# Attention on pairs of heads, with float32 weights and a column of ones in the first layer

## The chip, the cores and the metric

The kernel runs on one core of one Trainium2 chip. The metric is the device time of one execution in microseconds (us), the median of several runs. The engines are TensorE (PE for its matmuls, PEld for its weight loads), VectorE (DVE), ScalarE (ACT), GpSimd (POOL) and SyncE (SP, which issues DMAs). They run their own instruction streams and meet at semaphores.

## The reference, cut to what matters

Two layers, each a cross attention and a mixture of experts, over 8 batches of 112 tokens with 256 channels. The attention looks at 375 context tokens of 192 channels. Both attentions have 16 heads.

```python
# layer 0: 16 heads of 16 channels; scores are clamped to +-10000
q, k, v = y @ Wq + bq, ctx @ Wk + bk, ctx @ Wv + bv
s = clip(q_h @ k_h.T * 0.25, -CLAMP, CLAMP)
o_h = softmax(s) @ v_h
x = x + tanh(g) * (concat(o_h) @ Wo + bo)
# layer 1: 16 heads of 64 channels, low-rank additions to the four weights;
# the last 4 context tokens have their own keys, values and softmax,
# and their result is added to that of the other 371
```

## The kernel before

Activations and weights are kept as pairs of float16 values, a high and a low part ("hi" and "lo"), and a product is made of three matmuls, hi·hi, hi·lo and lo·hi (`PARTS`). ACT writes the high part out of PSUM (a copy to float16), DVE the low part (PSUM minus the high part).

The span has these stages: set-up and weight cutting, attention of layer 0, its experts, weights of layer 1, attention of layer 1, its experts. `attention_tensor` (L537), `attention_scalar` (L688), `attention_vector` (L771) and `attention_gpsimd` (L914) are called once for each layer, and each writes out by hand one engine's order of work. The loop is over batches, and inside it over the 16 heads. For a head:

- `scores` (L603): PE makes the 112x375 scores (371 in layer 1) in three matmuls (L613) into one of two PSUM banks, `SB_[st % 2]`. The contraction runs over all 128 partitions. In layer 0 one tile of keys holds 8 heads of 16 channels, so the queries of a head lie in `qz` with zeros for the other seven heads; POOL writes them (`masks`, L917, four multiplications by a mask for each batch, L921). In layer 1 one tile holds two heads and the other half of the rows is zero.
- `maxima` (L835): in layer 0 DVE clamps the scores into `SC` and takes the extreme value along (L844), and clips once more (L847). In layer 1 it only takes the negated maximum (L850).
- `exps` (L719): ACT makes the exponentials into `P_` (float32) and sums them along (L728; the sum is a second instruction, ACTIVATION_READ_ACCUMULATOR). In layer 1 POOL then writes the 4 values of the special tokens beside them (L939).
- `turn` (L617): PE transposes the 112x375 float32 values in three pieces of 125 keys (L623), two heads after `scores`.
- `hi` (L732) and `lo` (L853): ACT and DVE cut the transposed values to a high and a low float16 part (L736, L855).
- `weigh` (L627): PE multiplies each piece, both parts, with the high and low values of the head side by side (L640), six matmuls a head, three heads after `scores`.
- `normalise` (L859): when a group of heads is done (all 16 in layer 0, four in layer 1), DVE adds the halves and multiplies by the reciprocal of the sum (L866 to L874).

Beside the heads stand "units" (`Layer.steps`), the work on the next batch's queries ("q"), keys ("k"), values ("v") and, in layer 1, special tokens ("i"), and on the last batch's result (transposes "t", product "o"). The table in `Layer.__init__` says behind which head each unit stands. A unit is PE's matmuls into one of the two banks `GB` (L558 for q, with the bias in one-row matmuls L564 in layer 0; L570 for k; L576 for v; L584 for i; L591 for t; L597 and the one-row bias L600 for o), and then ACT's and DVE's copies out. In layer 0 there are one q, two k, three v, one t and one o for a batch; in layer 1 two q, eight k, one i, six v, two t and one o.

Of the kernel before, what the change touches and what calls it, by code (L numbers as in the profile page):

```python
# [38 lines left out]
OS = 16.0  # L39
SQ, DEG = 2, 8  # L40
# [14 lines left out]
NORM_LAG = (3, 3)  # L55
# [9 lines left out]
class Layer:  # L65


    def __init__(self, index, dim):
# [12 lines left out]
        self.v_units = [("v", c, w) for c in range(NCH) for w in range(self.width // self.vw)]  # L81
# [28 lines left out]
def acts(u):  # L110

    return u[0] not in ("i", "o")


def build(nc, a, out):
    ctx = ExitStack()
    with ctx:
# [3 lines left out]
        def sem(name):  # L121
# [25 lines left out]
        P_ = flat[0:S, 0:2 * KV].rearrange("p (a n) -> p a n", a=2)  # L147
        SC = flat[0:S, 768:768 + 2 * KV].rearrange("p (a n) -> p a n", a=2)
        OB = flat[0:S, 1536:1536 + 1024]
        PT = flat[0:CHUNK, 2560:2560 + 2 * NCH * S].bitcast(F16)\  # L150
            .rearrange("p (a q c n) -> p a q c n", a=2, q=2, c=NCH)
        OT = flat[:, 3328:3328 + 8 * S].bitcast(F16).rearrange("p (q t n) -> p q t n", q=2, t=8)
        qu = flat[:, 4352:4352 + 4 * S].bitcast(F16).rearrange("p (a q t n) -> p a q t n", a=2, q=2, t=2)
        mask = sb("mask", [128, 8], F16)

        qflat = qz[:, :, :, :, :].rearrange("p a q h n -> p (a q h n)")
        hf = qflat[:, 0:8 * HT].bitcast(F32).rearrange("p (a n) -> p a n", a=HB)
# [35 lines left out]
        pb = [ctx.enter_context(nc.psum_tensor(f"pb{i}", [128, 512], F32)) for i in range(8)]  # L193
# [38 lines left out]
        names = """x_in small_in ident_set const_set ones_set below_set eyes_set  # L232
# [6 lines left out]
        for L in range(2):  # L239
            for n in """s_mm clip_done mx_done exp_done t_mm hi_done lo_done pv_mm g_mm g_hi g_free  # L240
                    qz_done o_rd r_done x_up ipa_patch ipa_sc ipa_z ipa_m ipa_e ipa_s ipa_r ipa_pn vi_in""".split():
                s[f"{n}{L}"] = sem(f"{n}{L}")
# [12 lines left out]

        LD = VF[0:3 * RANK, 0:DOWN_N + UP_N]
# [280 lines left out]
        def attention_tensor(pe, L):  # L537
# [11 lines left out]
            def unit(kind, u, n, ns, bv, bs, behind=1):  # L549
# [21 lines left out]
                elif u[0] == "v":  # L571
# [31 lines left out]
            def scores(bv, bs, h):  # L603
                i, st = bv * H + h, bs * H + h
                if h == 0:
                    pe.wait_ge(g_free, front_done(L, bv, bs, "k"))
                    if l == 0:
                        pe.wait_ge(s["qz_done0"], 4 * bv + 4)
                if st >= 2:

                    pe.wait_ge(s["mx_done0"] if l == 0 else s["exp_done1"], i - 1)
                for n, (qa, qb) in enumerate(PARTS):
                    mm = pe.matmul(SB_[st % 2][0:S, 0:L.keys], qz[:, bs % 2, qa, h, :],  # L613
                                   kT[bs % 2][qb][:, h // L.per_tile, 0:L.keys], start=(n == 0), stop=(n == 2))
                mm.then_inc(s[f"s_mm{l}"], 1)

            def turn(i, st):  # L617

                pe.wait_ge(s["exp_done0"] if l == 0 else s["ipa_patch1"], i + 1)
                if st >= 2:  # L620
                    pe.wait_ge(s[f"lo_done{l}"], i - 1)
                for c in range(NCH):
                    mm = pe.transpose(TB_[st % 2][0:CHUNK, c * S:(c + 1) * S],  # L623
                                      P_[:, st % 2, c * CHUNK:(c + 1) * CHUNK], identf[0:S, 0:S])
                mm.then_inc(s[f"t_mm{l}"], 1)

            def weigh(bv, bs, h):  # L627
                i, st = bv * H + h, bs * H + h
                if h == 0:
# [3 lines left out]
                group, gs = bv * L.groups + h // L.grouped, bs * L.groups + h // L.grouped  # L633
                if h % L.grouped == 0 and gs >= 2:
                    pe.wait_ge(s[f"o_rd{l}"], group - 1)
                pe.wait_ge(s[f"lo_done{l}"], i + 1)
                for c in range(NCH):

                    for qa in range(2):
                        mm = pe.matmul(psum_out(L, gs, h), PT[:, st % 2, qa, c, :],  # L640
                                       V[0:CHUNK, bs % 2, :, c, h * L.dim:(h + 1) * L.dim],
                                       start=(c == 0 and qa == 0), stop=(c == NCH - 1 and qa == 1))
                mm.then_inc(s[f"pv_mm{l}"], 1)

            def batch(where, bv, bs):
# [4 lines left out]
                for h in range(H):  # L650
                    scores(bv, bs, h)
                    if bs or h >= 2:
                        turn(bv * H + h - 2, bs * H + h - 2)
                    if bs or h >= 3:
                        if h >= 3:
                            weigh(bv, bs, h - 3)
                        else:
                            weigh(bv - 1, bs - 1, H + h - 3)
                    for hh, kind, u, n, ns, _ in todo:
                        if hh == h:  # L660
                            d = 1 if kind == "front" else -1
                            unit(kind, u, n, ns, bv + d, bs + d, behind)

            for _, kind, u, n, ns, _ in prologue_units(L):
                unit(kind, u, n, ns, 0, 0)
            batch("first", 0, 0)
# [5 lines left out]
            for i in range(B * H - 2, B * H):  # L672
                turn(i, i)
# [1154 lines left out]
```

## Time and profile before

| what | value |
|---|---|
| median of 3 runs | 1280.2 us (1274.51 to 1282.06) |
| span of the profiled execution | 1277.4 us |
| PE busy | 1066.5 us (83%) |
| DVE busy | 948.8 us (74%) |
| ACT busy | 567.6 us (44%) |
| POOL busy | 268.6 us (21%) |

The profiled execution is another than the timed ones; its span is 2.8 us below their median, and a sum made in it is carried over by that difference. Matmuls are pipelined, so the duration of one in the profile includes its way through the array; what it costs in a row of others is the distance from one start to the next.

### The profile page before, as it was taken

What the parts mean: (1) busy time and instruction counts of PE and PEld (TensorE: products, weight loads), DVE (VectorE), ACT (ScalarE), POOL (GpSimd) and SP (SyncE); (2) the same over time, 40 slices, a digit from 0 to 9 for tenths busy, and PEclk for the clock granted to TensorE, in tenths of its full rate; (3) what the DMA queues carried; (4) which work ended last, traced back from release to release, by engine and by line L of the source; (5) the groups of instructions that cost most, each with busy time, mean ns of one, the idle gap of its engine ahead of it and who ended that gap; (6) DMA issues with size and microseconds to landing.
All of it is one profiled execution on the core that took longest, in us unless ns stands there. A gap on an engine that the chain in (4) does not pass through costs nothing.

```text
span 1277.4 us, 23029 instructions
## 1 busy us (share of the span) xinstructions
PE 1066.5 (83%) x7860; PEld 746.0 (58%) x7860; DVE 948.8 (74%) x2024; ACT 567.6 (44%) x1276; POOL 268.6 (21%) x303
## 2 busy tenths in 40 slices
PE   0688888882979999854688988998897699999997
PEld 0577777771634555643367877777776455455553
DVE  5588888897398888697567777777776667776775
ACT  3366666672433343441455556555555233222220
POOL 1422222202245563001000000000000013433331
PEclk9899999995699999896799999999998699999999
DMA  5000000001112122320000000000000231112100
GB/s 190 1 2 2 1 0 0 0 1 66 64 48 84 58 96 67 110 71 28 6 1 2 2 2 1 1 0 1 1 1 1 100 129 64 64 64 72 70 1 29
DMA packets 9935, 47.82 MB, mean 37 GB/s; under 512 B 1513, under 2 KB 3313, under 8 KB 6930
## 3 DMA queue, kind: packets, MB, share of 16 engines
q1 hardware_dynamic: 9874, 47.03, 10.7%
q8 instruction: 36, 0.59, 0.2%
q14 instruction: 25, 0.20, 0.1%
HBM read 45.92 MB, written 1.11 MB: 37 GB/s over the span
## 4 chain that ended last, share of the span: by engine, by line
PE 33%; DVE 30%; issue 20%; ACT 9%; POOL 5%; DMA 2%; DVEq 1%; ACTq 0%; POOLq 0%
PE pb L1119 8%; PE pb L1134 7%; POOL qz L1227 5%; DVE ST L844 4%; DVE ST L855 3%; DVE nm L850 3%; PE pb L640 2%; PE pb L613 2%; PE pb L597 2%; DVE ST L847 2%; ACT ST L728 2%; PE pb L1424 2%; PE pb L576 1%; ACT V L711 1%; PE pb L570 1%
## 5 line engine op out<-in xcount | busy, mean ns | idle before, releaser
L1119 PE MATMUL pb<-xT,KT 128*128 128x448 f16 x1248 | 244.2, 354 | 2.7 <-DVE qz L1197 2.7
L1227 POOL TENSOR_TENSOR qz<-qz,Z 128x448 f32<-128x448 f32 x128 | 169.1, 1331 | 286.8 <-ACT qz L1166 197.5
L1119 PEld LDWEIGHTS pb<-xT,KT 128*128 128x128 f16 x1248 | 121.6, 98 | 119.6 <-DVE qz L1197 5.8
L613 PE MATMUL pb<-KT,qz 128*112 128x375 f16 (+1 forms) x768 | 171.8, 334 | 3.2 <-POOL qz L921 2.1
L640 PE MATMUL pb<-V,ST 125*112 125x32 f16 (+1 forms) x1536 | 127.0, 214 | 53.2 <-DVE ST L855 52.9
L1134 PE MATMUL pb<-V,KT 128*128 128x448 f16 x816 | 162.6, 357 | 8.9 <-DVE V L1206 8.9
L640 PEld LDWEIGHTS pb<-V,ST 125*112 125x112 f16 x1536 | 109.9, 133 | 71.3 <-DVE ST L855 47.2
L736 ACT ACTIVATE ST<-pb 125x336 f16<-125x336 f32 x256 | 113.6, 444 | 45.1 <-PE pb L623 42.5
L855 DVE SCALAR_TENSOR_TENSOR ST<-pb,ST 125x336 f16<-125x336 f32 x256 | 127.7, 499 | 6.0 <-ACT ST L736 5.4
L1134 PEld LDWEIGHTS pb<-V,KT 128*128 128x128 f16 x816 | 80.3, 99 | 86.3 <-DVE V L1206 10.5
L623 PE MATMUL pb<-identf,ST 112*125 112x112 f32 x768 | 125.8, 273 | 1.6 <-ACT ST L728 1.6
L623 PEld LDWEIGHTS pb<-identf,ST 112*125 112x125 f32 x768 | 120.0, 193 | 9.8 <-ACT ST L728 1.9
L1206 DVE TENSOR_TENSOR V<-qz,V 128x448 f16<-128x448 f32 x136 | 117.3, 863 | 4.7
L728 ACT ACTIVATE ST<-pb,nm 112x371 f32<-112x371 f32 x128 | 72.9, 569 | 104.1 <-DVE nm L850 104.1
L1204 DVE CAST V<-qz 128x448 f16<-128x448 f32 x136 | 94.9, 698 | 23.2 <-POOL qz L1227 19.5
L1166 ACT ACTIVATE qz<-pb 128x448 f32<-128x448 f32 x72 | 39.1, 543 | 158.9 <-PE pb L1119 158.9
L728 ACT ACTIVATE ST<-ST,nm 112x375 f32<-112x375 f32 x128 | 77.8, 608 | 69.4 <-DVE ST L847 69.3
L613 PEld LDWEIGHTS pb<-KT,qz 128*112 128x112 f16 x768 | 91.5, 134 | 26.0 <-issue 5.8
L939 POOL TENSOR_TENSOR ST<-pn,sums 112x4 f32<-112x4 f32 x128 | 25.5, 200 | 352.3 <-ACT ST L728 352.3
L921 POOL TENSOR_TENSOR qz<-ST,mask 128x896 f16<-128x896 f16 x32 | 55.0, 1749 | 183.9 <-DVE ST L783 183.9
L1197 DVE SCALAR_TENSOR_TENSOR qz<-pb,qz 128x448 f32<-128x448 f32 x72 | 44.5, 618 | 53.9 <-POOL qz L1227 50.7
L791 DVE SCALAR_TENSOR_TENSOR KT<-pb,KT 128x371 f16<-128x371 f32 (+1 forms) x80 | 43.6, 544 | 42.6 <-ACT KT L707 42.6
(196 smaller groups left out, 1594.0 us busy)
## 6 DMA issues: line engine op xcount, KB each, us to landing
ST<-in_moe SPq DMA_DIRECT2D x9, 1536.0 KB, 7.8
ST<-in_moe SPq DMA_DIRECT2D x8, 1024.0 KB, 6.8
Z<-wd_scratch SPq DMA_DIRECT2D x16, 448.0 KB, 4.4
ST<-in_ctxT SPq DMA_DIRECT2D x4, 750.0 KB, 4.9
ST<-in_gens SPq DMA_DIRECT2D x2, 768.0 KB, 4.7
ST<-in_lora SPq DMA_DIRECT2D x2, 624.0 KB, 8.7
ST<-in_w1q SPq DMA_DIRECT2D x1, 1024.0 KB
ST<-in_w1k SPq DMA_DIRECT2D x1, 1024.0 KB
```

Of the source, the lines that this page charges most:

```text
L613: mm = pe.matmul(SB_[st % 2][0:S, 0:L.keys], qz[:, bs % 2, qa, h, :], kT[bs % 2][qb][:, h // L.per_tile, 0:L.keys], start=(n == 0), stop=( ...
L623: mm = pe.transpose(TB_[st % 2][0:CHUNK, c * S:(c + 1) * S], P_[:, st % 2, c * CHUNK:(c + 1) * CHUNK], identf[0:S, 0:S])
L640: mm = pe.matmul(psum_out(L, gs, h), PT[:, st % 2, qa, c, :], V[0:CHUNK, bs % 2, :, c, h * L.dim:(h + 1) * L.dim], start=(c == 0 and qa == ...
L728: act.activation(P_[:, st % 2, 0:L.keys], src, ACT.Exp, bias=nm[:, st % 4:st % 4 + 1], scale=1.0 if l else -1.0, accum_out=sums[:, bs % 2, ...
L736: act.activation(PT[:, st % 2, 0, :, :], TB_[st % 2][0:CHUNK, 0:NCH * S] .rearrange("p (c n) -> p c n", c=NCH), ACT.Copy).then_inc(s[f"hi_ ...
L855: dve.scalar_tensor_tensor(PT[:, st % 2, 1, :, :], TB_[st % 2][0:CHUNK, 0:NCH * S] .rearrange("p (c n) -> p c n", c=NCH), 1.0, PT[:, st % ...
L921: pool.tensor_tensor(qz[:, bs % 2, q, 8 * t:8 * t + 8, :], bc(qu[:, bs % 2, q, t, :].unsqueeze(1), [128, 8, S]), bc(mask[:, :].unsqueeze(2 ...
L1119: mm = pe.matmul(banks[m % len(banks)][:, 0:HT], MW[:, es % 2, qa, c:c + 128], xT[:, qb, k, half * HT:(half + 1) * HT], start=(i == 0), st ...
L1134: mm = pe.matmul(SUM[half][c][:, 0:HT], MW[:, es % 2, qa, c0:c0 + 128], HTt[:, half, qb, k, :], start=False, stop=(es == n - 1 and i == last))
L1204: dve.tensor_copy(HTt[:, half, 0, m, :], hf[:, m % HB, :]).then_inc(s[f"u_hi_{l}"], 1)
L1206: dve.tensor_tensor(HTt[:, half, 1, m, :], hf[:, m % HB, :], HTt[:, half, 0, m, :], ALU.subtract).then_inc(s[f"u_lo_{l}"], 1)
L1227: pool.tensor_tensor(tile, tile, wdB[:, es % 2, half * HT:(half + 1) * HT], ALU.mult)\
```

## The change

Both layers go over pairs of heads (`NP` = 8 steps a batch). Layer 0 takes the pairs (0,2), (4,6), (1,3), (5,7) and the same for heads 8 to 15, layer 1 takes neighbours. One step's scores use both PSUM banks, one for each head of the pair; the three matmuls of the two heads alternate, and each uses only the rows that hold its head: 32 of 128 partitions in layer 0, 64 in layer 1. In layer 0 a block of 32 rows holds an even and an odd head, and the queries are kept in two versions, one with the odd heads' rows zero and one with the even heads' (`par` is a scale that is zero on those rows), written by ACT and DVE straight from PSUM; POOL's masks are gone. The clip (L847), the maximum of layer 1 (L850), `hi` and `lo` become one instruction for a pair. POOL's L939 too.

In layer 0 the transposed exponentials stay float32 (`PT0`), the values too (`V0`, with a 17th column of ones for each head), `lo` is empty, the sums along L728 are gone, and `weigh` is three float32 matmuls of 17 columns for a head. `normalise` reads the sum from the 17th column and is two instructions. Scores are issued one step ahead, at the end of the step before.

```diff
+        order = [0, 2, 4, 6, 1, 3, 5, 7]
+        self.order = list(range(H)) if index else order + [8 + h for h in order]
+        self.pairs = [self.order[2 * p:2 * p + 2] for p in range(NP)]
...
+            def scores(bv, bs, p):
+                i, st = bv * NP + p, bs * NP + p
...
+                if st >= 1:
+                    pe.wait_ge(s["mx_done0"] if l == 0 else s["exp_done1"], 2 * i)
                 for n, (qa, qb) in enumerate(PARTS):
-                    mm = pe.matmul(SB_[st % 2][0:S, 0:L.keys], qz[:, bs % 2, qa, h, :],
-                                   kT[bs % 2][qb][:, h // L.per_tile, 0:L.keys], start=(n == 0), stop=(n == 2))
+                    for j, h in enumerate(L.pairs[p]):
+                        if l == 0:
+                            t, r = h // 8, slice(32 * (h % 8 // 2), 32 * (h % 8 // 2) + 32)
+                            q = qv[r, bs % 2, h % 2, qa, t, :]
+                        else:
+                            t, r = h // 2, slice(64 * (h % 2), 64 * (h % 2) + 64)
+                            q = qz[r, bs % 2, qa, h, :]
+                        mm = pe.matmul(SB_[j][0:S, 0:L.keys], q, kT[bs % 2][qb][r, t, 0:L.keys],
+                                       start=(n == 0), stop=(n == 2))
...
+                if l == 0:
+                    pe.wait_ge(s["exp_done0"], 2 * i + 2)
+                else:
+                    pe.wait_ge(s["ipa_patch1"], i + 1)
+                if st >= 1:
+                    pe.wait_ge(s["lo_done1"] if l else s["hi_done0"], i)
+                for j in range(2):
+                    for c in range(NCH):
+                        mm = pe.transpose(TB_[j][0:CHUNK, c * S:(c + 1) * S],
+                                          P_[:, st % 2, j, c * CHUNK:(c + 1) * CHUNK], identf[0:S, 0:S])
...
+                for j, h in enumerate(L.pairs[p]):
+                    for c in range(NCH):
+                        if l == 0:
+                            mm = pe.matmul(psum_out(L, gs, h), PT0[:, st % 2, j, c * S:(c + 1) * S],
+                                           V0[0:CHUNK, bs % 2, c, h, :], start=(c == 0), stop=(c == NCH - 1))
+                            continue
...
+                for p in range(NP):
+                    if bs or p >= 1:
+                        turn(bv * NP + p - 1, bs * NP + p - 1)
+                    if p >= 2:
+                        weigh(bv, bs, p - 2)
+                    elif bs:
+                        weigh(bv - 1, bs - 1, NP + p - 2)
                     for hh, kind, u, n, ns, _ in todo:
-                        if hh == h:
+                        if hh // 2 == p:
...
+                    if p < NP - 1:
+                        scores(bv, bs, p + 1)
+                    elif where != "last":
+                        scores(bv + 1, bs + 1, 0)
...
                 if u[0] == "q" and l == 0:
-                    act.activation(qu[:, bs % 2, 0, :, :], bank[:, 0:2 * S].rearrange("p (t n) -> p t n", t=2),
-                                   ACT.Copy, scale=QSCALE[0]).then_inc(g_hi, 1)
+                    for v in range(2):
+                        x = act.activation(qv[:, bs % 2, v, 0, :, :], bank[:, 0:2 * S].rearrange("p (t n) -> p t n", t=2),
+                                           ACT.Copy, scale=par[:, v:v + 1])
...
+                if l == 0:
+                    act.activation(P_[:, st % 2, j, :], src, ACT.Exp, bias=nm[:, c:c + 1], scale=-1.0)\
+                        .then_inc(s["exp_done0"], 1)
+                    return
...
+                act.activation(PT[:, st % 2, :, 0, :] if l else PT0[:, st % 2, :, :], TP2[0:CHUNK, :, 0:NCH * S], ACT.Copy)\
+                   .then_inc(s[f"hi_done{l}"], 1)
...
+                    for j in range(2):
+                        exps(bv, bs, p, j)
+                        for hh, kind, u, n, ns, nh in todo:
+                            if hh == 2 * p + j:
...
+                elif u[0] == "w":
+                    x = dve.tensor_scalar(V0[0:CHUNK, bs % 2, u[1], :, 0:16],
+                                          bank[0:CHUNK, 0:C].rearrange("p (h d) -> p h d", h=H), 1.0 / WS, None,
+                                          ALU.mult)
...
+                    for j in range(2):
+                        dve.tensor_scalar(SC[:, st % 2, j, :], SB_[j][0:S, 0:L.keys], -CLAMP, CLAMP, ALU.max, ALU.min,
+                                          accum_out=nm[:, c + j:c + j + 1]).then_inc(s["mx_done0"], 1)
+                    dve.wait_ge(s["mx_done0"], 2 * i + 2)
+                    dve.tensor_scalar(SC[:, st % 2, :, :], SC[:, st % 2, :, :], CLAMP, None, ALU.min)\
                        .then_inc(s["clip_done0"], 1)
...
+                dve.tensor_reduce(nm[:, c:c + 2], SP2[0:S, :, 0:L.keys], AX.X, ALU.max, negate=True)\
                    .then_inc(s[f"mx_done{l}"], 1)
...
             def lo(i, st):
+                if l == 0:
+                    return
...
+                if l == 0:
+                    whole = OBK[gs % 2][0:S, 0:H * 17].rearrange("p (h d) -> p h d", h=H)
+                    dve.reciprocal(rinv[:, heads], whole[:, :, 16]).then_inc(s["r_done0"], 1)
+                    dve.wait_ge(s["r_done0"], group + 1)
+                    dve.tensor_tensor(ob, whole[:, :, 0:16], bc(rinv[:, heads].unsqueeze(2), [S, H, 16]), ALU.mult)\
+                       .then_inc(s["o_rd0"], 1)
+                    return
...
+            pool.memset(V0[:, :, :, :, 16], 1.0).then_inc(s["ones_col"], 1)
...
-            attention_gpsimd(pool, layers[0])
...
+            dve.wait_ge(s["ident_set"], 5)
+            dve.tensor_reduce(par[:, :], mask[:, :].rearrange("p (j v) -> p v j", v=2), AX.X, ALU.add)\
+               .then_inc(s["par_set"], 1)
+            dve.wait_ge(s["par_set"], 1)
+            dve.tensor_scalar(par[:, :], par[:, :], QSCALE[0], None, ALU.mult).then_inc(s["par_set"], 1)
```

## Rows read from the trace of the kernel before

**Rows 1.** The page: span, and busy time of each engine.

```profile
span 1277.4 us, 23029 instructions
...
PE 1066.5 (83%) x7860; PEld 746.0 (58%) x7860; DVE 948.8 (74%) x2024; ACT 567.6 (44%) x1276; POOL 268.6 (21%) x303
```

**Rows 2.** The chain that ended last, in order of time (start us, us, what).

```profile
294.06 1.50 PE pb L597 x6
...
757.17 1.61 PE pb L584 x32
...
801.53 1.61 PE pb L584 x32
```

**Rows 3.** Stretches: length, busy us of PE, PEld, DVE, ACT, POOL; PEclk, DMA share, GB/s.

```profile
152.00:183.00 31.00, 27.23 (x249) 23.18 (x247) 26.92 (x78) 19.57 (x55) 6.92 (x4) 0.94 0.00 0
755.00:800.00 45.00, 41.14 (x383) 33.55 (x381) 33.52 (x78) 26.28 (x71) 3.23 (x17) 1.00 0.00 1
```

**Rows 4.** Groups by line and shape, first layer: busy us, mean ns | idle before.

```profile
L855 DVE SCALAR_TENSOR_TENSOR ST<-pb,ST 125x336 f16<-125x336 f32 x256 | 127.7, 499 | 6.0 <-ACT ST L736 5.4
...
L736 ACT ACTIVATE ST<-pb 125x336 f16<-125x336 f32 x256 | 113.6, 444 | 45.1 <-PE pb L623 42.5
...
L728 ACT ACTIVATE ST<-ST,nm 112x375 f32<-112x375 f32 x128 | 77.8, 608 | 69.4 <-DVE ST L847 69.3
...
L844 DVE TENSOR_SCALAR_CACHE_REDUCE ST<-pb 112x375 f32<-112x375 f32 x128 | 68.9, 538 | 3.3 <-PE pb L613 2.4 <-ACT ST L728 0.6
...
L921 POOL TENSOR_TENSOR qz<-ST,mask 128x896 f16<-128x896 f16 x32 | 55.0, 1749 | 183.9 <-DVE ST L783 183.9
...
L728 ACT ACTIVATION_READ_ACCUMULATOR ST<-ST,nm 112x1 f32 x128 | 23.9, 186 | 0.0
...
L844 DVE DVE_READ_ACCUMULATOR ST<-pb 112x1 f32 x128 | 10.4, 81 | 0.0
```

**Rows 5.** One line alone, L847: ns min/median/max.

```profile
L847 DVE TENSOR_SCALAR ST<-ST x128: 354/356/1474, 49.2 to 287.7; 112x375 f32<-112x375 f32 x128
```

**Rows 6.** Timeline of PE, first layer, 158 to 162 us.

```profile
158.82 0.64 PE L613 MATMUL pb<-KT,qz 128*112 128x375 f16 x3
159.30 0.48 PE L623 MATMUL pb<-identf,ST 112*125 112x112 f32 x3
159.61 0.44 PE L640 MATMUL pb<-V,ST 125*112 125x32 f16 x6
159.90 0.84 PE L597 MATMUL pb<-W,ST 128*112 128x256 f16 x6
160.67 0.42 PE L600 MATMUL pb<-RW,ones 1*112 1x256 f16 x2
```

**Rows 7.** Timeline of PEld, same stretch.

```profile
160.67 0.17 PEld L600 LDWEIGHTS pb<-RW,ones 1*112 1x112 f16 x2 [0.18 <-issue]
161.02 0.34 PEld L613 LDWEIGHTS pb<-KT,qz 128*112 128x112 f16 x3 [0.18 <-issue]
```

**Rows 8.** Timeline of PE, second layer, 714 to 724 us.

```profile
714.33 0.66 PE L613 MATMUL pb<-KT,qz 128*112 128x371 f16 x3
714.83 0.48 PE L623 MATMUL pb<-identf,ST 112*125 112x112 f32 x3
715.15 0.50 PE L640 MATMUL pb<-V,ST 125*112 125x128 f16 x6
715.48 1.25 PE L576 MATMUL pb<-W,cT 128*125 128x512 f16 x5
716.57 2.78 PE L597 MATMUL pb<-W,ST 128*112 128x256 f16 x24
```

**Rows 9.** Groups by line and shape, second layer.

```profile
L728 ACT ACTIVATE ST<-pb,nm 112x371 f32<-112x371 f32 x128 | 72.9, 569 | 104.1 <-DVE nm L850 104.1
...
L850 DVE TENSOR_REDUCE nm<-pb 112x1 f32<-112x371 f32 x128 | 68.6, 536 | 0.6
```

**Rows 10.** Timeline, start of the first layer.

```profile
47.95 0.66 PE L613 MATMUL pb<-KT,qz 128*112 128x375 f16 x3 [2.08 <-POOL qz L921]
```

More of the change, by code:

```diff
@@ L39 @@
 OS = 16.0
+NP = H // 2
 SQ, DEG = 2, 8
@@ L80, in __init__ @@
         self.k_units = [("k", t) for t in range(self.tiles)]
-        self.v_units = [("v", c, w) for c in range(NCH) for w in range(self.width // self.vw)]
+        self.v_units = [("v" if index else "w", c, w) for c in range(NCH) for w in range(self.width // self.vw)]
         self.i_units = [("i",)] if index else []
@@ L191, in build @@
         zz = sb("zz", [S, 3, B])
-        pb = [ctx.enter_context(nc.psum_tensor(f"pb{i}", [128, 512], F32)) for i in range(8)]
+        SP2 = ctx.enter_context(nc.psum_tensor("sp", [128, 2, 512], F32))
+        TP2 = ctx.enter_context(nc.psum_tensor("tp", [128, 2, 512], F32))
+        pb = [SP2[:, 0, :], SP2[:, 1, :], TP2[:, 0, :], TP2[:, 1, :]] + \
+             [ctx.enter_context(nc.psum_tensor(f"pb{i}", [128, 512], F32))[:, :] for i in range(4, 8)]
         SB_, TB_, OBK, GB = pb[0:2], pb[2:4], pb[4:6], pb[6:8]
@@ L632, in weigh @@
                         pe.wait_ge(s[f"vi_in{bs % 2}"], (bv - bs % 2) * 16 + 32)
-                group, gs = bv * L.groups + h // L.grouped, bs * L.groups + h // L.grouped
-                if h % L.grouped == 0 and gs >= 2:
+                group, gs = bv * L.groups + 2 * p // L.grouped, bs * L.groups + 2 * p // L.grouped
+                if 2 * p % L.grouped == 0 and gs >= 2:
                     pe.wait_ge(s[f"o_rd{l}"], group - 1)
[L636 to L642, printed above, removed]
+                pe.wait_ge(s["lo_done1"] if l else s["hi_done0"], i + 1)
+                for j, h in enumerate(L.pairs[p]):
[4 more added lines that the diff above has]
+                            continue
+                        for qa in range(2):
+                            mm = pe.matmul(psum_out(L, gs, h), PT[:, st % 2, j, qa, c * S:(c + 1) * S],
+                                           V[0:CHUNK, bs % 2, :, c, h * L.dim:(h + 1) * L.dim],
+                                           start=(c == 0 and qa == 0), stop=(c == NCH - 1 and qa == 1))
                 mm.then_inc(s[f"pv_mm{l}"], 1)
@@ L649, in batch @@
                 behind = at[L.out[-1]] - at[L.out[-2]] if at else 1
[L650 to L658, printed above, removed]
+                for p in range(NP):
[5 more added lines that the diff above has]
+                        weigh(bv - 1, bs - 1, NP + p - 2)
                     for hh, kind, u, n, ns, _ in todo:
-                        if hh == h:
+                        if hh // 2 == p:
                             d = 1 if kind == "front" else -1
                             unit(kind, u, n, ns, bv + d, bs + d, behind)
+                    if p < NP - 1:
+                        scores(bv, bs, p + 1)
+                    elif where != "last":
+                        scores(bv + 1, bs + 1, 0)
             for _, kind, u, n, ns, _ in prologue_units(L):
                 unit(kind, u, n, ns, 0, 0)
+            scores(0, 0, 0)
             batch("first", 0, 0)
@@ L671, in attention_tensor @@
             batch("last", B - 1, B - 1)
-            for i in range(B * H - 2, B * H):
-                turn(i, i)
-                weigh(B - 1, B - 1, i - 1 - (B - 1) * H)
-            weigh(B - 1, B - 1, H - 1)
+            turn(B * NP - 1, B * NP - 1)
+            weigh(B - 1, B - 1, NP - 2)
+            weigh(B - 1, B - 1, NP - 1)
             for _, kind, u, n, ns, _ in tail_units(L):
@@ L765, in attention_scalar @@
             batch("last", B - 1, B - 1)
-            for i in range(B * H - 2, B * H):
-                hi(i, i)
+            hi(B * NP - 1, B * NP - 1)
             for _, kind, u, n, ns, nh in tail_units(L):
@@ L782, in unit @@
                 if u[0] == "q" and l == 0:
-                    x = dve.scalar_tensor_tensor(qu[:, bs % 2, 1, :, :],
-                                                 bank[:, 0:2 * S].rearrange("p (t n) -> p t n", t=2), QSCALE[0],
-                                                 qu[:, bs % 2, 0, :, :], *step)
+                    for v in range(2):
+                        x = dve.scalar_tensor_tensor(qv[:, bs % 2, v, 1, :, :],
+                                                     bank[:, 0:2 * S].rearrange("p (t n) -> p t n", t=2),
+                                                     par[:, v:v + 1], qv[:, bs % 2, v, 0, :, :], *step)
                 elif u[0] == "q":
@@ L907, in attention_vector @@
             batch("last", B - 1, B - 1)
-            for i in range(B * H - 2, B * H):
-                lo(i, i)
+            lo(B * NP - 1, B * NP - 1)
             normalise(B - 1, B - 1, L.groups - 1)
```

181 lines of the change are left out of this document (76 added, 105 removed).

## The prediction

> **What bounds the kernel now.** I read the page first: PE is busy for 83% of the span and DVE for 74% [rows 1], but the change touches only the two attention stages, so both have to be read there. The chain in order of time gives their lengths. The first scores start at 47.95 us [rows 10] and the last output product of layer 0 at 294.06, so layer 0 takes about 246 us, 30.8 a batch. In layer 1 the special-token matmuls of two following batches start at 757.17 and 801.53 [rows 2]: 44.3 us a batch, some 355 in all.
>
> The two windows show who is short in each. In 31 us of layer 0 DVE is busy 26.9 us and PE 27.2; in 45 us of layer 1 PE is busy 41.1 and DVE 33.5 [rows 3]. PE's busy time holds the way through the array, so I rebuild it from starts. In layer 0 [rows 6] three score matmuls take 0.48 us (158.82 to 159.30), three transposes 0.31, six weighing matmuls 0.29. With 16 heads that is 17.3 us. The units: k ten matmuls of 0.16 (1.6), v fifteen of 0.11 (the L597 form, 0.77 for six and a step to another form, has the same 256 columns; 1.6), o 1.1, q about 1.1, t 0.2, together 5.6. So PE needs 22.9 of 31 us. DVE's union is 26.9 of 31: layer 0 is DVE's, with waits between the engines. For layer 1 [rows 8]: scores 0.50, transposes 0.32, weighing 0.33, 18.2 for 16 heads; the units are k 40 matmuls of 0.16 (6.4), v 30 of 0.22 (1.09 for five; 6.5), o 2.8, i 32 matmuls in 1.6, q 48 small ones in 2.4, t 0.8: 20.5. PE needs 38.7 of 44.3 us: layer 1 is PE's.
>
> **Layer 0, what goes from DVE and ACT.** Each head loses L855 (0.499 us, 16 a batch) on DVE [rows 4]. The durations overlap the next instruction's by up to 0.1, so I take 0.41: 6.6 us a batch. The clip of two heads in one instruction saves its fixed part, about 0.1 of 0.35, for eight: 0.8. L847 has a median of 0.356 but a mean of 0.472 in the groups and a maximum of 1.474 [rows 5]; the long ones lie beside POOL's masks (L921, four of 1.749 a batch [rows 4]), which go, so (0.472-0.356)·16 = 1.9. `normalise` loses two of four instructions (0.8), q gains one (0.4), v loses none. DVE falls from 26.9 by 9.7 to about 17. ACT loses 16 sums of 0.186 (3.0), the v copies (1.1), and pays 8·0.78 instead of 16·0.444 for `hi` (0.9 less): from 19.6 to about 15. Neither bounds layer 0 afterwards. PE does, or the round through all engines.
>
> **Scores.** Two heads of a step use different rows and alternate. If the two run beside each other, three distances of 0.16 remain of six: 0.48 saved a pair. But the trace shows what a step to another number of rows costs. Before the one-row matmuls L600 and again after them PEld stands for 0.18 us with no wait [rows 7], and L597 to L600 takes 0.77 for six where six of 0.11 are 0.66: about 0.1 on each side. From 160.67 to the next scores at 161.02 there are 0.35 us, for two matmuls of 0.11 and one step back of 0.1, so that also each small load within such a form is no longer hidden. So for a pair: three times (0.16 + 0.05), and twice 0.1, is 0.8 us against 0.96 before; bounds 0.66 (loads hidden) and 1.16 (nothing side by side). I take 0.8, 1.3 us less a batch, in both layers.
>
> The row shows the stand at the one-row form. The Trainium skill, "TensorEngine Tiling (Array Packing)", section Key Properties, says that changing the tiling mode drains TensorE, while tiles work independently; by that rule the 0.18 of the row comes twice for each pair here, and it speaks against the change's gain in layer 1.
>
> **Float32 weighing.** This is the term that decides, and no row shows it. The nearest are the float32 transposes: 0.31/3 = 0.103 us each with a load of 125 columns [rows 6]; a load of 112 columns would be 0.092 to 0.096. The float16 weighing has two loads of 0.05 for a piece. The new one has a single matmul of 17 columns for a piece, 48 a batch. Lower end: it costs one load like the transposes', 0.1, 48·0.1 = 4.8 us against 96·0.05 = 4.8 before: nothing. Upper end: float32 weights and values each have to be taken in two parts, four combinations, each with a load of its own at 0.096: 0.384, 18.4 us. In between: two such loads with two short streams behind each, or four loads at the float16 distance of 0.05: 0.2, 9.6 us. I take 0.2. It is the nearest to both rows at once, four times the 0.05 of the matmul that is replaced (same 112 columns, nearly as few streamed) and twice the 0.1 of the float32 load.
>
> The row shows 0.103 for one pass of the transposes. The Trainium skill, "FP8 and Floating Point Precision", section TensorE Precision Notes, states that true FP32 takes four passes through the array. If each pass has the transposes' load, this is the 0.384 case, a rival below; if only the stream is repeated, it is mine. No trace here shows which.
>
> **Layer 0, the sum.** PE for a batch: scores 8·0.8 = 6.4, transposes 48·0.103 = 5.0, weighing 9.6, units 5.6: 26.6, 3.3 a pair. The round: from the issue of a pair's scores 0.8, their way out 0.15, two clamps 1.2 (2·(0.538+0.081) less overlap), the clip 0.55, two exponentials of 0.608 [rows 4], and three handovers of 0.1, together 4.2 to 4.3; then PE's `turn` of this pair 0.62, `weigh` of the pair before 1.2, units 0.7, and only then the scores after the next. That is two steps in 6.8 us, so no step is under 3.4. PE and the round are nearly equal, and I take 3.5 a pair: 28.0 us a batch against 30.8, 22 us for eight batches.
>
> At the start PE stood 2.08 us for the masks [rows 10], and DVE's first clips beside them took over 1 us; 3 us go there. Costed at nothing: the setting of `par` on DVE and of the ones on POOL, which lie in the wait for x at the start; if that cover is gone it is under 1 us.
>
> **Layer 1, the sum.** DVE and ACT save little (one L850 for two heads, about 0.15 a pair, `lo` 0.15 and `hi` 0.1), and PE only 1.3 us a batch. What is new is a tighter round: both score banks belong to one pair, so the next scores wait for both exponentials of this pair, where they waited for that of the head two back. ACT does the first exponential, then a unit, then the second; that unit's matmuls come on PE only after `turn` and `weigh`. From one scores to the next therefore: scores 0.8, wait for POOL's patch 0.3, `turn` 0.64, `weigh` 0.67, the unit's matmuls a, handover and copy 0.75, the second exponential 0.76 (0.569 and the sum's 0.19 [rows 9]), handover 0.1: 4.0 + a. Or PE's own sum, 2.4 and all units of the step, where that is more. With a = 1.2 for q, 0.8 for k, 1.1 for v: steps 0 to 7 take 5.2 and a second ACT piece of 0.5, 4.8, 4.9, 4.8, 4.8, 7.9 (i, v and o, PE's own), 5.1, 5.7: 43.7 against 44.3. I take 5 us less in eight batches. The bounds: scores at 0.66 and rounds that overlap better, 42 a batch (18 less); scores at 1.16 and the special unit's exponential late, 46.5 (18 more).
>
> **The forecast.** 1277.4 - 22 - 3 - 5 = 1247.4 in the profiled execution, 1250 at the median, which lies 2.8 higher. It is named after its decisive term, float32 weighing at about 0.2. Its own range is 1225 to 1268.
>
> **Rivals.**
> 1. The float32 matmul loads four times at 0.096. PE for a batch of layer 0: 6.4 + 5.0 + 18.4 + 5.6 = 35.4, with waits 36.5, 5.7 more than before, 46 in eight batches. Time 1280.2 + 46 - 3 - 5 = 1318. PE becomes the bound where DVE was; it decides from 0.26 us a float32 matmul on, where layer 0 comes out even. For it: a 4-byte load already takes twice the 2-byte one a column [rows 6]. Against it: the stream is only 17 columns, and nothing in the trace shows a repeated load.
> 2. One pass: 0.1 a matmul. The round then sets 3.2 a pair, 25.6 a batch, 41 less: 1280.2 - 41 - 8 = 1231.
> 3. The pair step is paid back by waits: the tighter round costs layer 1 18 us more, and layer 0 keeps half its gain: 1280.2 + 18 - 11 - 3 = 1284, no change. For it: ACT waits 104.1 us for L850 already [rows 9] and PE's clock in layer 0 is 0.94, so it falls to 1.2 GHz for part of each batch when PE stands [rows 3]; rounds with more standing would have more of that. Against: PE's share in layer 1 is high and its clock 1.00.
>
> **How the numbers follow.** Forecast 0.47, rival 1 0.33, rival 2 0.09, rival 3 0.11. A measurement here tells about 1% from no change. Faster by over 1% (under 1267): nearly all of the forecast, rival 2 and nothing else, 0.55. Within 1%: an edge of the forecast and most of rival 3, 0.11. Slower by over 1%: rival 1 and the bad edge of rival 3, 0.34. The range 1218 to 1322 reaches to rival 1's value, as it has a third of the chance, and down past rival 2's.
>
> **What would show it.** Right: the distance between float32 weighing matmuls in `weigh` near 0.2, with up to four records for each; layer 0 at 28 us a batch, DVE under 19 busy in it; a score pair's six matmuls within 0.6 and PEld standing near 0.1 to 0.18 before and after; layer 1 at 43 to 44.5 a batch, with PE waiting for L728's second exponential before the scores. Wrong: PE's weighing at 2 us or more a pair (rival 1), no stand at all and scores within 0.5 (layer 1 then gains more), or layer 1 over 45.

## The result and the profile after

The changed kernel takes 1405.2 us (median of 4 runs, 1393.7 to 1405.8) against 1279.6; the ratio is 1.097, 95% interval 1.092 to 1.101. The forecast was 1250 and the range ended at 1322. It is 125 us slower, and neither the range nor a rival held it.

The page of the changed kernel, as in [rows 1], with the row of the granted clock in 40 slices of 35 us (tenths of full speed) added:

```profile
span 1402.9 us, 21584 instructions
...
PE 1213.0 (86%) x7860; PEld 833.9 (59%) x7860; DVE 868.1 (62%) x1698; ACT 530.3 (38%) x1004; POOL 202.5 (14%) x208
...
PEclk9755555555555699999977999999999879999998
```

PE's share is higher than before, and in eleven slices in a row the clock is 5 tenths (70 to 456 us). They are the attention of layer 0, which ends at 430.9 us, and the first 25 us of its experts. The same two windows as in [rows 3], one batch of each layer (length, busy us of PE, PEld, DVE, ACT, POOL with instructions, then PEclk, DMA share and GB/s):

```profile
167.00:216.00 49.00, 48.46 (x246) 38.83 (x245) 17.16 (x51) 15.77 (x29) 0.00 (x0) 0.50 0.00 0
892.50:935.00 42.50, 38.30 (x377) 28.38 (x377) 32.12 (x61) 24.92 (x61) 1.64 (x8) 1.00 0.00 1
```

In layer 0 PE is busy for 48.46 of 49 us, at a clock of 0.50 throughout; DVE has fallen to 17.2 us and ACT to 15.8, as forecast, and POOL is empty. In layer 1 the clock is 1.00 and PE busy for 38.3 us. The chain gives layer 1's period, as [rows 2] did:

```profile
843.03 1.62 PE pb L596 x32
...
885.69 1.61 PE pb L596 x32
```

That is 42.7 us a batch against 44.3. For layer 0 I took the distance between VectorE's additions of the output product of two batches: 48.96 us against 30.6 to 30.8. The whole difference of the two profiled executions adds up from the ends of the stages: up to the end of layer 0's attention +135.2 us, from there to the end of layer 1's -10.9, after it +1.2, together 125.5 (1402.9 - 1277.4). Of the 10.9, 9.0 lie between layer 1's first scores and its last addition (339.2 us against 348.2).

Where the clock falls can be read on PE's timeline at the start of the layer (start us, duration, engine, line, operation, count):

```profile
46.38 0.68 PE L630 MATMUL sp<-KT,qz 32*112 32x375 f16 x6
46.99 0.47 PE L570 MATMUL pb<-xT,W 128*128 128x112 f16 x6
...
50.58 1.60 PE L644 MATMUL tp<-identf,ST 112*125 112x112 f32 x6 [1.71 <-ACT ST L760]
51.97 1.77 PE L582 MATMUL pb<-cT,WKV 128*128 128x375 f16 x5
53.68 1.19 PE L630 MATMUL sp<-KT,qz 32*112 32x375 f16 x6
54.79 1.60 PE L644 MATMUL tp<-identf,ST 112*125 112x112 f32 x6
56.19 2.29 PE L661 MATMUL pb<-V,ST 125*112 125x17 f32 x12
58.31 1.73 PE L582 MATMUL pb<-cT,WKV 128*128 128x375 f16 x5
```

Six score matmuls take 0.61 us at 46.38 (to 46.99), and 1.11 at 53.68 (to 54.79), with nothing else changed: between them the clock went from 2.4 to 1.2 GHz. The six transposes from 50.58 are already at the lower level, 1.39 us to the next where [rows 6] make it 0.62. From there on PE shows hardly a gap, and the clock does not come back before the layer is over. PE had been busy without a break from 46.38 to 48.86 and had then stood for 1.71 us.

The fall itself is not what is new. The kernel before falls to 1.2 GHz at 53.9 us, too, and is back at 2.4 at 60.7, with PE at work on the same layer. The same two windows, first of the kernel before, then of the changed one:

```profile
56.00:60.00 4.00, 4.00 (x19) 2.99 (x18) 2.62 (x7) 2.05 (x5) 1.99 (x2) 0.50 0.02 4
62.00:90.00 28.00, 22.93 (x223) 19.83 (x221) 24.09 (x70) 17.73 (x51) 6.92 (x4) 1.00 0.01 1
```

```profile
56.00:60.00 4.00, 4.00 (x21) 2.89 (x20) 0.52 (x1) 1.72 (x3) 0.00 (x0) 0.50 0.00 0
62.00:90.00 28.00, 28.00 (x143) 23.70 (x141) 9.92 (x31) 8.73 (x16) 0.00 (x0) 0.50 0.00 1
```

PE is busy for 4.00 of 4 us in both at 56 us; at 62 us the kernel before is at 1.00 and the changed one still at 0.50, where it stays up to 476.9 us. So what has to be explained is why the clock does not come back. The means of the changed kernel's groups show the low clock as well (busy us, mean ns of one):

```profile
L644 PE MATMUL tp<-identf,ST 112*125 112x112 f32 x768 | 161.2, 364 | 6.5 <-ACT ST L760 5.0 <-POOL ST L970 1.5
...
L661 PE MATMUL pb<-V,ST 125*112 125x17 f32 x768 | 146.4, 339 | 0.0
...
L630 PE MATMUL sp<-KT,qz 32*112 32x375 f16 x384 | 74.9, 523 | 0.0
...
L630 PE MATMUL sp<-KT,qz 64*112 64x371 f16 x384 | 44.1, 336 | 29.1 <-ACT ST L763 29.1
```

The 32-row scores take 523 ns each, the 64-row ones of layer 1 336. L661 has 768 records where the program has 384 float32 matmuls: each comes as two loads and two matmuls.

### The profile page after: what moved, and what is told of

Same layout as the page of the kernel before. It is cut to its first block, busy times and chain, and to the rows that moved or that the text cites. A ratio compares the mean times of both kernels' runs of the same rounds, so it can differ in the third digit from the quotient of the medians.

```text
span 1402.9 us, 21584 instructions
## 1 busy us (share of the span) xinstructions
PE 1213.0 (86%) x7860; PEld 833.9 (59%) x7860; DVE 868.1 (62%) x1698; ACT 530.3 (38%) x1004; POOL 202.5 (14%) x208
## 3 DMA queue, kind: packets, MB, share of 16 engines
HBM read 45.92 MB, written 1.11 MB: 34 GB/s over the span
## 4 chain that ended last, share of the span: by engine, by line
PE 58%; DVE 15%; issue 12%; ACT 7%; POOL 4%; DMA 2%; DVEq 0%; POOLq 0%; ACTq 0%
PE tp L644 10%; PE pb L661 10%; PE sp L630 6%; PE pb L1165 6%; POOL qz L1258 4%; PE pb L588 4%; PE tp L1150 4%; PE sp L1150 4%; PE pb L582 3%; PE pb L609 3%; PE pb L665 2%; ACT ST L763 2%; DVE nm L890 1%; PE pb L570 1%; DVE KT L1519 1%
## 5 line engine op out<-in xcount | busy, mean ns | idle before, releaser
L770 ACT ACTIVATE ST<-tp 125x672 f32<-125x672 f32 (+1 forms) x128 | 93.6, 731 | 297.0 <-PE tp L644 297.0
L644 PEld LDWEIGHTS tp<-identf,ST 112*125 112x125 f32 x768 | 132.6, 257 | 58.8 <-issue 47.6
L644 PE MATMUL tp<-identf,ST 112*125 112x112 f32 x768 | 161.2, 364 | 6.5 <-ACT ST L760 5.0
L661 PEld LDWEIGHTS pb<-V,ST 125*112 125x112 f32 x768 | 150.9, 307 | 0.0
L661 PE MATMUL pb<-V,ST 125*112 125x17 f32 x768 | 146.4, 339 | 0.0
L630 PE MATMUL sp<-KT,qz 32*112 32x375 f16 (+1 forms) x768 | 119.0, 429 | 29.1 <-ACT ST L763 29.1
L1150 PE MATMUL tp<-xT,KT 128*128 128x448 f16 x624 | 133.6, 355 | 2.7 <-DVE qz L1228 2.7
L1150 PE MATMUL sp<-xT,KT 128*128 128x448 f16 x624 | 135.4, 358 | 0.0
L884 DVE TENSOR_SCALAR_CACHE_REDUCE ST<-sp 112x375 f32<-112x375 f32 x128 | 65.0, 546 | 76.4 <-PE sp L630 76.3
L1235 DVE CAST V<-qz 128x448 f16<-128x448 f32 x136 | 95.8, 705 | 21.9 <-POOL qz L1258 18.2
L763 ACT ACTIVATE ST<-sp,nm 112x371 f32<-112x371 f32 x128 | 72.6, 568 | 13.8 <-DVE nm L890 13.3
```

Of the source, the lines that this page charges most:

```text
L630: mm = pe.matmul(SB_[j][0:S, 0:L.keys], q, kT[bs % 2][qb][r, t, 0:L.keys], start=(n == 0), stop=(n == 2))
L644: mm = pe.transpose(TB_[j][0:CHUNK, c * S:(c + 1) * S], P_[:, st % 2, j, c * CHUNK:(c + 1) * CHUNK], identf[0:S, 0:S])
L661: mm = pe.matmul(psum_out(L, gs, h), PT0[:, st % 2, j, c * S:(c + 1) * S], V0[0:CHUNK, bs % 2, c, h, :], start=(c == 0), stop=(c == NCH - 1))
L763: act.activation(P_[:, st % 2, j, 0:L.keys], src, ACT.Exp, bias=nm[:, c:c + 1], scale=1.0, accum_out=sums[:, bs % 2, h:h + 1]).then_inc(s[ ...
L770: act.activation(PT[:, st % 2, :, 0, :] if l else PT0[:, st % 2, :, :], TP2[0:CHUNK, :, 0:NCH * S], ACT.Copy)\
L884: dve.tensor_scalar(SC[:, st % 2, j, :], SB_[j][0:S, 0:L.keys], -CLAMP, CLAMP, ALU.max, ALU.min, accum_out=nm[:, c + j:c + j + 1]).then_in ...
```

## Experiments

Ten kernels ran. e2, e3, e4, e5 and e8 have one execution each, the others four to seven; the kernel before took 1271.9 to 1282.1 us in all of its executions but one (5851 us, left out), so a single time tells no less than 10 us. Theory A is that the loss is the clock of layer 0 alone; A1 and A2 name the 32-row scores or the float32 weighing as what holds it down.

**Layer 0 as before, layer 1 as in the change (e1).** Both layers' functions stand side by side, and each engine calls the old ones for layer 0.

```diff
-            attention_tensor(pe, layers[0])
+            attention_tensor_b(pe, layers[0])
...
-            attention_vector(dve, layers[0])
+            attention_vector_b(dve, layers[0])
```

> Layer 0 works as before (heads one by one, masks by GpSimd, float16 weighing), layer 1 as in the change. Theory A (the clock of layer 0 carries the whole loss, layer 1 is a gain of 1.7 us a batch of its own): layer 0 back at 30.7 us a batch with a granted clock of about 0.94, layer 1 at 42.6 a batch, time about 1280 - 13 = 1267. Rival (the pairs of layer 1 gain only because of something layer 0 leaves behind, or not at all): 1280.

1270.5 us, ratio 0.994 (0.992 to 0.996), as theory A had it. Layer 1 takes 42.6 us a batch, layer 0 is back at 30.6 to 30.8. One of its batches:

```profile
160.00:191.00 31.00, 25.61 (x247) 21.92 (x246) 26.84 (x77) 19.78 (x56) 6.92 (x4) 1.00 0.00 0
```

The clock is 1.00 here, and from 58.4 us to the end of the layer, where the kernel before has 0.94 [rows 3], at the same period. So the short stretches at 1.2 GHz that the kernel before shows in each batch of layer 0 cost it nothing. Layer 1's gain stands by itself, 1.7 us a batch, and the loss comes from the change to layer 0.

**Scores of layer 0 over all 128 rows (e2).** The selection of one head is left out, so that the scores are sums over four heads.

```diff
-                            q = qv[r, bs % 2, h % 2, qa, t, :]
+                            q, r = qv[:, bs % 2, h % 2, qa, t, :], slice(0, 128)
```

> The change, but the scores of layer 0 contract over all 128 rows with the queries of four heads at once (the selection of one head is left out, so the scores are sums over four heads); the number and length of the matmuls stay. Theory A1 (TensorE stays at 1.2 GHz because the score matmuls use only 32 rows): the clock in layer 0 returns to 2.4 GHz for most of it, layer 0 falls from 49 to about 29 us a batch, time about 1250. Theory A2 (the float32 weighing keeps the clock down): the clock stays at 0.5 in layer 0 and the six score matmuls of a pair no longer run side by side, 0.9 us more a pair, time about 1450.

1257.7 us, as A1 had it. One batch, and PE's timeline in it:

```profile
150.00:178.80 28.80, 28.30 (x245) 24.99 (x244) 17.07 (x51) 16.37 (x29) 0.00 (x0) 1.00 0.00 0
```

```profile
166.58 1.12 PE L630 MATMUL sp<-KT,qz 128*112 128x375 f16 x6
167.53 0.81 PE L644 MATMUL tp<-identf,ST 112*125 112x112 f32 x6
168.18 1.26 PE L661 MATMUL pb<-V,ST 125*112 125x17 f32 x12
169.29 0.96 PE L582 MATMUL pb<-cT,WKV 128*128 x5
```

The clock is 1.00, a batch takes 28.8 us. Everything of the change but the row number is in this kernel; its scores are other numbers, and e9 below has the right ones at the same clock. The twelve records of one pair's float32 weighing last 1.11 us (168.18 to 169.29), 0.185 for each matmul. Six scores take 0.95, since they no longer run side by side.

**Float16 weighing in one go (e3).** `V0` and `PT0` are float16 instead of float32, one matmul a piece; the low parts are left out.

```diff
-        V0 = VF[:, 0:4 * NCH * H * 17].bitcast(F32).rearrange(...)
+        V0 = VF[:, 0:2 * NCH * H * 17].rearrange(...)
...
```

> The change, but the values and exponentials of layer 0 that are weighed are float16, with one matmul of 17 columns a piece (their low parts are left out). Theory A1 (32-row scores keep the clock down): the clock stays at 0.5, and each piece takes 0.1 us instead of 0.37, 13 us less a batch at the most: about 36 us a batch, time about 1300. Theory A2 (float32 weighing keeps the clock down): clock back to 2.4 GHz, layer 0 at 24 us a batch or less, time about 1210.

1294.8 us, near A1's number. A batch in the later part of layer 0:

```profile
239.00:276.00 37.00, 36.03 (x198) 26.31 (x197) 17.17 (x51) 15.96 (x30) 0.00 (x0) 0.50 0.00 0
```

The clock is still 0.50, with not one float32 matmul in the weighing. It was not so from the start: the second to fourth batch take 30.2 to 33.1 us, with the clock changing level several times up to 172 us, the later ones 36.8. Between 125 and 141 us it was at full speed with the 32-row scores:

```profile
125.00:141.00 16.00, 12.65 (x120) 9.46 (x119) 11.11 (x35) 9.56 (x17) 0.00 (x0) 1.00 0.00 1
```

So A1 holds for most of the layer, not for every stretch of it.

**More full matmuls beside it (e4).** Three matmuls of 128 rows and 240 columns for a pair, into columns that nobody reads.

```diff
+                if l == 0:
+                    pe.matmul(OBK[gs % 2][:, 272:512], W0[:, 0, 0:128], cT[:, 0, 0, 0:240], start=True, stop=True)
...
```

> The change with three float16 matmuls more for each pair in layer 0, 128 rows and 240 columns each, ahead of the weighing, into columns of PSUM that nobody reads. They are 0.6 us a pair at 1.2 GHz and 0.3 at 2.4. Theory A (the engine is granted 1.2 GHz because what it does in layer 0 counts as too little work, though its records leave no gap): with more of full matmuls the clock rises for at least a part, layer 0 falls below 49 us a batch although work was added. Rival (the clock is down for another reason, not the amount of work): it stays at 0.5 and layer 0 takes 49 + 8 * 0.6 = 54 us a batch, time about 1445.

1453.5 us, near the rival's number (1445; two batches of layer 1 took 4 and 5 us more here than in the other runs, which is not explained):

```profile
233.00:286.80 53.80, 53.26 (x269) 42.55 (x268) 17.19 (x52) 15.76 (x29) 0.00 (x0) 0.50 0.00 0
```

53.8 us a batch, still at 0.50: 4.8 more for the 24 added matmuls, 0.2 each. Work of another kind beside the 32-row scores did not bring the clock back, at least in this amount.

**The kernel before with 32-row scores (e5).** One part of the change alone. The queries are masked already, so the values are the same.

```diff
+                r = slice(0, 128) if l else slice(32 * (h % 8 // 2), 32 * (h % 8 // 2) + 32)
                 for n, (qa, qb) in enumerate(PARTS):
-                    mm = pe.matmul(SB_[st % 2][0:S, 0:L.keys], qz[:, bs % 2, qa, h, :],
-                                   kT[bs % 2][qb][:, h // L.per_tile, 0:L.keys], start=(n == 0), stop=(n == 2))
+                    mm = pe.matmul(SB_[st % 2][0:S, 0:L.keys], qz[r, bs % 2, qa, h, :],
+                                   kT[bs % 2][qb][r, h // L.per_tile, 0:L.keys], start=(n == 0), stop=(n == 2))
```

> The kernel before with one edit: the scores of layer 0 contract over the 32 rows that hold the head instead of all 128 (the other rows hold zeros, so the values are the same). No pairs, no float32 weighing. Theory A1 (scores on 32 rows are enough to be granted 1.2 GHz): the clock falls to 0.5 for most of layer 0, which takes over 40 us a batch, time about 1360. Rival (32 rows hold the clock down only together with the float32 weighing): clock about 0.94, 16 * 0.2 = 3 us a batch more for the changes of form, time about 1305.

1432.6 us: the clock falls as A1 had it, and the time is beyond both expectations. One batch, and a part of PE's timeline:

```profile
226.00:276.50 50.50, 50.50 (x244) 35.89 (x245) 29.17 (x77) 19.55 (x55) 6.81 (x4) 0.50 0.00 0
```

```profile
239.54 1.19 PE L614 MATMUL pb<-KT,qz 32*112 32x375 f16 x3
240.66 0.97 PE L624 MATMUL pb<-identf,ST 112*125 112x112 f32 x3
241.42 0.70 PE L641 MATMUL pb<-V,ST 125*112 125x32 f16 x6
242.05 1.19 PE L614 MATMUL pb<-KT,qz 32*112 32x375 f16 x3
```

The clock is 0.50 and PE has no gap in 50.5 us. Three scores take 1.12 us (239.54 to 240.66) where [rows 6] have 0.48, the transposes 0.76 for 0.31, the weighing 0.63 for 0.29. Not all of that is the clock. In its own short stretch at 1.2 GHz the kernel before has

```profile
57.35 1.14 PE L613 MATMUL pb<-KT,qz 128*112 128x375 f16 x3
58.29 0.81 PE L623 MATMUL pb<-identf,ST 112*125 112x112 f32 x3
58.89 0.70 PE L640 MATMUL pb<-V,ST 125*112 125x32 f16 x6
59.43 1.17 PE L613 MATMUL pb<-KT,qz 128*112 128x375 f16 x3
```

0.94, 0.60 and 0.54 us for the three, 0.43 less a head, so the changes of form are some 7 of the 50.5 us. No pairs, no float32 weighing, no side-by-side matmuls: the row number alone does it. With e2 and e9, in which the whole change runs at full clock on all rows, this settles which part of the change is the cause.

**Eight versions of the queries with 128 rows (e6), and four versions with 64 rows (e7).** Both compute the reference, without GpSimd's masks.

```diff
-        par = sb("par", [128, 2])
+        par = sb("par", [128, 8])
...
-                            t, r = h // 8, slice(32 * (h % 8 // 2), 32 * (h % 8 // 2) + 32)
-                            q = qv[r, bs % 2, h % 2, qa, t, :]
+                            t, r = h // 8, slice(0, 128)
+                            q = qv[r, bs % 2, h % 8, qa, t, :]
```

In e7 the lines read `slice(64 * (h % 8 // 4), 64 * (h % 8 // 4) + 64)` and `h % 4`, and the pairs are (0,4), (1,5), (2,6), (3,7).

> The change with the queries of layer 0 in eight versions instead of two (each with one head of a tile and zeros elsewhere) and scores over all 128 rows, so that the whole computation is done. ScalarE and VectorE write six more versions a batch, 6 * 0.34 and 6 * 0.38 us. Theory A1: clock 1.0 in layer 0, 28.8 us a batch plus at most 2 for the longer q unit, time 1258 to 1272. Rival (the small time of the run with all rows came from its unselected scores): the clock is down, over 1350.

1300.2 us, ratio 1.018 (1.014 to 1.022): neither number. 34.1 us a batch:

```profile
139.00:173.10 34.10, 31.58 (x245) 27.42 (x244) 19.14 (x58) 18.49 (x35) 0.00 (x0) 0.90 0.00 0
```

The eight copies of the q unit stand in ACT's and DVE's order between the two exponentials of a pair and before the next clamps (durations, and in brackets the idle time before):

```profile
152.19 2.81 ACT L726 ACTIVATE qz<-pb,par 128x224 f16<-128x224 f32 x8 [0.40 <-PE pb L576]
...
155.04 2.96 DVE L818 SCALAR_TENSOR_TENSOR qz<-pb,par,qz 128x224 f16<-128x224 f32 x8 [3.97 <-ACT qz L726]
...
155.55 1.60 PE L644 MATMUL tp<-identf,ST 112*125 112x112 f32 x6 [2.31 <-ACT ST L760]
```

ACT's eight take 2.81 us and DVE's 2.96, one behind the other, PE stands for 2.31 us waiting for the exponentials, and with the transposes that follow (1.60 for six, where this kernel has 0.81 elsewhere) it is at 1.2 GHz. The clock's records have it there for 6.8 us in this batch and in all but one of the others. My expectation counted the copies as two us of busy time on engines with room; they are a wait on the round, and PE pays for it again in clock.

> As the run with eight versions, but four versions and scores over 64 rows, the two heads of a pair in different halves, so that they run side by side. If 64 rows are enough to keep 2.4 GHz, as they are in layer 1: 0.35 us less a pair than on 128 rows, 26 to 28 us a batch, time about 1245. If the clock falls (scores carry too little in layer 0, where PE has fewer full matmuls beside them): over 40 us a batch, 1350 or more.

1312.8 us, ratio 1.022 (1.016 to 1.028), by neither branch alone. The batches take 41.7, 30.2, 31.6, 33.9, 30.2 and 31.4 us. The first two of these:

```profile
111.00:153.00 42.00, 40.91 (x248) 32.76 (x247) 18.11 (x54) 16.86 (x31) 0.00 (x0) 0.62 0.01 1
153.00:183.00 30.00, 27.91 (x244) 22.40 (x243) 17.42 (x54) 16.99 (x31) 0.00 (x0) 0.94 0.00 0
```

With 64 rows the clock holds in one batch (0.94, 30.2 us) and not in the one before (0.62, 41.7 us). In layer 1 the 64-row scores keep 1.00, but there 20 of 38 us of PE's work are units on all rows by the prediction's sums, in layer 0 under 6 of 27.

**Layer 1 on all rows (e8).** On top of e6, whose layer 1 is the change's.

```diff
-                            t, r = h // 2, slice(64 * (h % 2), 64 * (h % 2) + 64)
+                            t, r = h // 2, slice(0, 128)
```

> As the run with eight versions, and the scores of layer 1 too contract over all 128 rows (the other half is zero). Theory (layer 1 gains by the side-by-side matmuls, 0.96 to 0.6 us a pair): 42.6 rises by 8 * 0.35 = 2.8 to 45.4 us a batch, above the 44.3 of before. Rival (it gains by pairs' fewer instructions on VectorE and ScalarE): under 43.5.

1304.8 us, against e6's 1300.2; 43.8 us a batch instead of 42.6, between the two expectations:

```profile
880.00:923.80 43.80, 40.35 (x377) 32.13 (x376) 32.45 (x61) 24.83 (x61) 1.64 (x8) 1.00 0.00 0
```

PE's busy time is 40.35 us against 38.30. So 1.2 of layer 1's 1.7 us come from the halves side by side and 0.5 from the rest of the pair step (fewer instructions, scores issued earlier), which no run tells apart. The expectation of 2.8 had left out the cost of the change of form: the net gain is 0.15 us a pair.

**The change with GpSimd's masks and 128 rows (e9), and with float16 weighing too (e10).**

```diff
-                            q = qv[r, bs % 2, h % 2, qa, t, :]
+                            q = qz[:, bs % 2, qa, h, :]
...
+            attention_gpsimd(pool, layers[0])
```

> The change with one part undone: GpSimd's masks come back, and the scores of layer 0 contract over all 128 rows of the masked queries, as before. Pairs and float32 weighing stay. Theory A1 (only the 32-row scores were bad, and the eight-version run lost its time to the long q unit): clock 1.0 in layer 0, 28.8 us a batch as in the run with all rows, up to 1 more for VectorE's clips beside the masks: time 1257 to 1266, a gain of 1 to 2% on before. Rival (the masks' or the pairs' waits bring the clock down as with eight versions): 34 us a batch, 1298.

1255.1 us, ratio 0.983 (0.981 to 0.986), a little under A1's 1257 to 1266: a version that keeps all of the change but one part is faster than both kernels.

```profile
span 1252.2 us, 21617 instructions
...
PE 1062.4 (85%) x7860; PEld 728.5 (58%) x7860; DVE 865.1 (69%) x1688; ACT 530.9 (42%) x996; POOL 259.9 (21%) x240
...
PEclk9999999985789999986899999999997699999998
```

```profile
150.00:178.80 28.80, 28.58 (x247) 25.24 (x246) 17.07 (x51) 15.93 (x28) 7.23 (x4) 1.00 0.00 0
```

28.5 us a batch at a clock of 1.00, PE busy for 28.6 of 28.8. POOL's masks (7.2 us) lie beside it, and DVE is at 17.1 us, so they cost nothing that can be seen. In both e2 and e9 the clock is at 1.00 already at the start of the layer.

> The same, and in layer 0 the weighing is as before too: high and low float16 parts, six matmuls of 32 columns a head, sums by ScalarE. It tells what float32 weighing does at 2.4 GHz. PE: 96 * 0.051 = 4.9 us a batch instead of 96 * 0.093 = 8.9; VectorE: 8 low parts of 0.85 and the values more, 8 us. If the round through the engines sets the pace (as in my sum), the float32 form and this one come out within 1 us a batch; if PE does, this one is 4 us a batch faster, 25 us a batch, time 1235; if VectorE does, it is slower, 30 us.

1272.6 us, ratio 0.996 (0.994 to 0.997), 30.3 us a batch, the time of the third branch:

```profile
150.00:180.00 30.00, 26.12 (x243) 20.65 (x243) 24.53 (x60) 17.81 (x47) 7.08 (x4) 1.00 0.00 0
```

At 2.4 GHz float32 weighing is thus worth 1.8 us a batch although it costs PE 4. DVE needs 24.5 us here and 17.1 with it, but neither it nor PE (26.1) fills the 30 us: PE waits for ACT's exponentials, and these for DVE's clips, 5.3 us in this window. So it is the round with DVE's longer part in it. Pairs alone, with the old weighing, bring layer 0 only 0.4 us a batch.

## Why the prediction was wrong

The step that failed is the one that was not worked out: "The sum" for layer 0 took PE's distances from rows at a clock of 0.94 and 1.00 [rows 3, 6] and kept them, and asked of the 32-row scores only what they cost in time (0.8 us a pair), not what they do to the clock of all matmuls around them. The runs show a clock of 0.50 in its place, and with it 49.0 us a batch for the 28.0 of the sum; on all rows the same kernel has 1.00 and 28.8 (e2) or 28.5 (e9). I read the 0.94 and gave it to rival 3, as a danger of standing still. In the change PE did not stand still: it was at 1.2 GHz while busy for 48.46 of 49 us. The Trainium skill, "TensorE: Matmul & The Clock Gate", Part 1, speaks of activity that releases the throttle and of idle gaps that bring it back. The first half this case bears out in part: what releases the clock in the kernel before (4.00 of 4 us busy at 56 us, 1.00 from 62 us on) does not do so in the change, though PE is as busy. The gaps are not in its trace, except the 1.71 us at its start.

The other steps, against the runs:

- Float32 weighing at 0.2 a matmul, between bounds of 0.1 and 0.384: 0.185 at 2.4 GHz (e2). In the change the next one starts 0.373 us after it, at 1.2 GHz, and a pair's six take 2.12 to 2.22. Rival 1 named 0.384 for another reason, four loads; the records have two loads a matmul. Its time of 1318 is missed as well, for it left the rest of PE at full speed.
- Scores at 0.8 us a pair with a change of form, 0.96 without: e8 against e6 gives 1.2/8 = 0.15 between them, as taken, for layer 1's 64 rows. In layer 0 a pair's six take 0.61 at 2.4 GHz and 1.12 at 1.2.
- PE's 26.6 us and the round's 3.5 a pair, 28.0 us a batch: e2 has 28.8 with 0.15 more for a pair's scores, e9 28.5. The same work at half the clock measured 49. No run has the 32-row scores at full clock for the whole layer; e2 and e9, whose scores cost more, take 1257.7 and 1255.1, both within the forecast's own range of 1225 to 1268. PE is busy for 28.58 of 28.8 us in e9, so of the two near-equal terms PE bounds, not the round.
- DVE at about 17 us and ACT at about 15: 17.2 and 15.8.
- Layer 1: 43.7 us forecast, 42.6 measured. The gain was right in sign, 9 us in all instead of 5. The round that I had feared does appear, as 29.1 us in which PE waits for the exponential before the scores, 3.6 a batch; PE's time had room for it.
- The start: the first scores come at 46.38 instead of 47.95, 1.6 us of the 3.
- Two small slips in the working, without weight: 16 heads of 0.50 + 0.32 + 0.33 are 18.4 us, not 18.2, and three distances of 0.16 with two changes of 0.1 are 0.68, not 0.66.

The signs of "wrong" that I listed would have shown it by accident: weighing at 2 us a pair is what the profile has (2.2), but as a sign of rival 1. A row of the clock stood in no sign.

What stays open: what in the matmuls of fewer rows keeps the clock at 1.2 GHz. e5 shows that 32 rows alone do it, e7 that 64 do it some of the time, e3 that with a shorter weighing the clock comes back twice, e4 that more other work, in the amount tried, does not help. A rival inside this is the change of form itself, which comes with every group of 32-row matmuls. It is not enough by itself, as layer 1 has the same two for each pair (its six scores take 0.61 us, too), at 64 rows and a clock of 1.00, but no run has 32-row scores without it. Fewer rows with more columns, or larger fillers, were not tried.

## What to carry to other kernels

Before putting matmuls on a part of the rows so that they run side by side, compare the granted clock, not only the distances: here 0.35 us a pair saved at 2.4 GHz cost 20 us a batch (49.0 against 28.8 in e2), because all of PE's work slowed down with it. Zero-padded queries on 128 rows look wasteful and were the faster form. And where one edit of several turns a gain into a loss, undo the parts one by one: the other parts (pairs in both layers, float32 weighing with the column of ones) were worth 1.7% together.

## What was not expected of the hardware

- TensorE stayed at 1.2 GHz for the whole of a layer while its records leave no gap (clock 0.50, PE 50.50 of 50.50 us busy in e5).
- A float32 matmul of 112 weight columns and 17 streamed columns takes 0.185 us at 2.4 GHz, as two loads and two matmuls, against 0.097 for two float16 loads with 32 columns each [rows 6: 0.29 for six].
- The two 32-row score matmuls of a pair, on different rows, start 3 to 5 ns apart in most records, and six of a pair take 0.61 us at 2.4 GHz against 0.95 on all rows.
- In layer 0 the kernel before spends some of each batch at 1.2 GHz at no cost: e1 has none of it after the first 10 us and the same period.
